# Constant matrix products on TensorE in two idle pieces of a router's first half

## The reference

```python
def reference(x, ctx, ...):
    x = x + slot_attention(layernorm(x), ctx, ...)   # 3 iterations: attention over 32 rows, GRU
    x = x + switch_ffn(layernorm(x), Wg, W1, W2)     # top-1 router, 8 experts
    return x

# the router of switch_ffn, capacity = 512 // 8 = 64
logits = einsum('bnd,de->bne', token_inputs, Wg)
gates = softmax(logits); expert_idx = argmax(gates)
mask = one_hot(expert_idx, 8)
pos = cumsum(mask, axis=1) * mask - mask             # position of the token within its expert
keep = mask * (pos < capacity)
dispatch = keep[..., None] * one_hot(pos, capacity)
expert_inputs = einsum('bnd,bnec->becd', token_inputs, dispatch)
h = gelu(einsum('becd,edh->bech', expert_inputs, W1))
expert_outputs = einsum('bech,ehd->becd', h, W2)
output = einsum('becd,bnec->bnd', expert_outputs, combine)   # combine = dispatch * gate
```

## Time and profile before

| | us |
|---|---|
| median of 3 runs | 147.22 |
| lowest and highest of them | 146.48, 147.29 |
| the profiled execution, whole | 146.29 |
| its span, first to last instruction | 144.5 |
| TensorE busy in the span | 123.9 (86%) |
| VectorE, ScalarE, GpSimd busy | 95.1, 80.3, 33.7 |

### The profile page before, as it was taken

The page is one execution under the profiler, slowest core; times in us unless marked ns, Lnnn a source line. Parts: engine busy times, 40 slices in busy tenths (PEclk is TensorE's granted clock), DMA queues, the critical chain, the costliest instruction groups (busy, mean ns, idle before and its releaser), DMA issues.

```text
span 144.5 us, 2709 instructions
## 1 busy us (share of the span) xinstructions
PE 123.9 (86%) x1007; PEld 92.4 (64%) x1007; DVE 95.1 (66%) x305; ACT 80.3 (56%) x156; POOL 33.7 (23%) x54
## 2 busy tenths in 40 slices
PE   0888999999899899899897833979999999999960
PEld 0684666575475484475474623769998889999730
DVE  2993992399698698796898899955359004124851
ACT  1646592676656746837834818927197246324540
POOL 5670913100500500401300033001400003773000
PEclk9999999999999999999999995599999999999996
DMA  3979970000000000000000000000011001113025
GB/s 110 272 235 351 396 278 0 0 0 2 5 0 0 0 0 0 5 0 2 0 5 0 0 0 0 0 0 5 2 36 39 27 12 40 49 48 93 1 71 145
DMA packets 9198, 8.05 MB, mean 56 GB/s; under 512 B 602, under 2 KB 7029, under 8 KB 9185
## 3 DMA queue, kind: packets, MB, share of 16 engines
q1 hardware_dynamic: 8492, 7.28, 15.5%
q0 software_dynamic: 256, 0.40, 1.1%
q10 hardware_dynamic: 436, 0.20, 0.5%
HBM read 6.43 MB, written 1.57 MB: 55 GB/s over the span
## 4 chain that ended last, share of the span: by engine, by line
PE 75%; ACT 11%; DVE 8%; DMA 2%; issue 1%; ACTq 0%
PE ps L1277 11%; PE ps L1291 11%; PE ps L1116 9%; PE ps L1097 7%; PE ps L1090 7%; PE ps L1198 7%; PE ps L1124 6%; ACT z_b L433 5%; PE ps L1303 3%; PE ps L1073 2%; DMA x_tok<-in_x_dram 2%; PE ps L995 2%; PE ps L1046 2%; PE ps L1056 1%; PE ps L983 1%
## 5 line engine op out<-in xcount | busy, mean ns | idle before, releaser
L1277 PE MATMUL ps<-h,W_t 128*128 128x128 f32 x128 | 16.0, 279 | 0.8 <-ACT h L469 0.8
L428 ACT ACTIVATE ps<-ps,half_b 128x512 f32<-128x512 f32 x12 | 7.9, 661 | 15.6 <-PE ps L1097 15.6
L1277 PEld LDWEIGHTS ps<-h,W_t 128*128 128x128 f32 x128 | 15.0, 192 | 1.8 <-issue 1.7
L1124 PE MATMUL ps<-attn,VW 32*128 32x256 f32 x144 | 12.9, 426 | 3.3 <-DVE ps L710 2.4
L1116 PE MATMUL ps<-h,whhT 128*128 128x256 f32 x48 | 13.5, 403 | 1.2 <-ACT z_b L433 1.2
L1097 PE MATMUL ps<-h,whhT 128*128 128x256 f32 x48 | 13.3, 398 | 0.0
L345 POOL DMA_INDIRECT y_tok<-y_rows,row_of x8 | 8.4, 1044 | 20.2 <-DMA y_rows<-y_sb 18.1
L710 DVE SCALAR_TENSOR_TENSOR ps<-r_b,ps 128x512 f32<-128x512 f32 x12 | 7.8, 693 | 7.6 <-ACT r_b L421 7.6
L1124 PEld LDWEIGHTS ps<-attn,VW 32*128 32x128 f32 x144 | 5.6, 182 | 10.2 <-DVE ps L710 4.8
L1116 PEld LDWEIGHTS ps<-h,whhT 128*128 128x128 f32 x48 | 8.2, 189 | 5.9 <-ACT z_b L433 3.2
L318 POOL TENSOR_SCALAR mse<-attn 128x8 f32<-128x8 f32 x6 | 1.2, 203 | 45.6 <-DVE attn L645 45.6
(11 more groups left out here) (166 smaller groups left out, 262.8 us busy)
## 6 DMA issues: line engine op xcount, KB each, us to landing
W_t<-in_L_ffn_W_dram SPq DMA_DIRECT2D x1, 2048.0 KB, 8.3
x_tok<-in_x_dram SPq DMA_DIRECT2D x4, 256.0 KB, 3.8
out_dram<-h SPq DMA_DIRECT2D x4, 256.0 KB, 2.3
y_rows<-y_sb SPq DMA_DIRECT2D x4, 128.0 KB, 1.8
n_b<-in_L_xattn_gru_whh_dram SPq DMA_DIRECT2D x1, 192.0 KB, 4.0
n_b<-in_L_xattn_gru_wih_dram SPq DMA_DIRECT2D x1, 192.0 KB, 3.8
y_tok<-y_rows,row_of POOLq DMA_INDIRECT x8, 2.5
n_b<-in_ctx_dram ACTq DMA_DIRECT2D x1, 64.0 KB, 2.9
```

Of the source, the lines that this page charges most:

```text
L428: nc.scalar.activation(HV[i], HV[i], ACT.Identity, bias=half_b[:, 2:3]).then_inc(s["hb"], 1)
L1124: last = mm(to[:, hf, :], VW[b][p:p + M, gate * P:(gate + 1) * P], attn[g][p:p + M, :], start=False, stop=True, skip_group_check=True)
L1277: last = mm(hid_bank[e][:, j * BG * CAP:(j + 1) * BG * CAP], W1_t[:, ex_, j * P:(j + 1) * P], rhs, start=True, stop=True)
```

## The change

TensorE gets a helper, `keep_clock(n, to)`, which issues n products of `ones_b` with its own first column, repeated 512 times, into bank `to`. Their results are not read. Five of them stand between `logits(1)` and `positions(0)`, and twelve between `positions(0)` and `dispatch(0)`, all into bank 7. At its start TensorE waits in addition until `ones_b` has been written.

```diff
@@ -972,6 +972,12 @@
             mm = nc.tensor.matmul
             tr = nc.tensor.transpose
 
+            def keep_clock(n, to=2):
+
+                for _ in range(n):
+                    mm(bank[to][:, 0:N], ones_b[:, :], ones_b[:, 0:1].broadcast_to([P, N]), start=True, stop=True)
+
+            pe.wait_ge(dve_set, 2)
             pe.wait_ge(pool_set, 4)
 
             def x_T(b):
@@ -1261,7 +1267,9 @@
             x2_back(1)
             logits(0)
             logits(1)
+            keep_clock(5, to=7)
             positions(0)
+            keep_clock(12, to=7)
             dispatch(0)
             dispatch(1)
 
```

## The result

The changed kernel takes 145.12 us (median of 4, 144.87 to 145.13); beside it the kernel before took 146.85 (median of 4, 146.44 to 147.29). The ratio is 0.9884, with a 95% interval of 0.9848 to 0.9920: 1.2% faster. The forecast was 145.8.

The account below looks back on a forecast made before the run. The prediction took TensorE's dispatch products, run partly at 1.2 GHz, to bound the kernel. Its terms 0 + 0 + 0 - 1.42 us took the median of 147.22 to 145.8 us, with an 8 in 10 range of 144.9 to 147.1.

Parts of the forecast that it names:

- cold products in the dispatch: 16 dispatch products on TensorE, partly at 1.2 GHz, last 6.3 us where about 4.2 us at full clock stand.
- The five and the twelve cost nothing: Five end at 85.2 us, before the mask; twelve end at 88.5, 0.4 us before dispatch(0): each adds 0.
- ScalarE takes over: Before up(0), ScalarE's two copies become the bound by 0.1 us; the second copy moves 1.42 us earlier.
- VectorE's rest for group 1: Rest before VectorE's group 1 work at 99.16 us: 3.02 us, of which 1.6 are left, so the gain stays.
- The profiled execution: Whole kernel in the traced execution: 146.29 us was to become 144.87 us.
- the last one: Step from profiled execution to median of runs: 147.22 us, 0.93 above the profiled one, minus 1.42 gives 145.8.
- would rather have lost more than this one: Argument against the partly saved rival: fewer cold dispatch products in the median execution, saving 0.7 us, 146.5 us, chance 0.16.
- The slow rivals: Clock falls further on, at up(0): 149.2 us, chance 0.07; or before the twelve products: 149.1 us, chance 0.05.
- the cold constants: Clock falls before the twelve, each takes 0.43 us, dispatch(0) starts at 90.8: 149.1 us, chance 0.05.

Follow-up runs that it names:

- the two edits on VectorE: Changed kernel with x2_shift(1) two one-hot tiles earlier on VectorE: 148.07 us; with scale_logits(0) also ahead of dispatch_hot(1): 147.76 us.
- VectorE's edit: Kernel before, without the constants, with x2_shift(1) two one-hot tiles of batch 0 earlier on VectorE: 151.10 us, ratio 1.0015.

## Why the prediction was right, point by point

- What bounds: cold products in the dispatch. Shown: full clock there and 1.49 us less in the stretch, the same in two traces on different chips; without the twelve the low clock and the 10.5 us are back, and with seventeen tiny products in place of the seventeen large ones, too.
- The five and the twelve cost nothing. That was right: `positions(0)` starts 0.06 us behind the mask's end as before, and the dispatch waits for ScalarE. Each takes 0.22 us, forecast 0.23; 0.60 us were spare, forecast 0.4.
- Batch 0 ends 2.13 us after its start and batch 1 2.06, forecast 2.09 each. Batch 1 starts 0.10 us behind x_hi(1), forecast 0.09.
- ScalarE takes over. Shown by its row without a gap and by the two edits on VectorE; with 8 of TensorE's products left out the stretch is still 9.01 us. The size was 1.42 us and is 1.49: I had added the copies end to end, but two in a row last 1.11 us together.
- VectorE's rest for group 1 was to shrink from 3.02 to 1.6 us. It is 1.52, and nothing ate the gain.
- The profiled execution: 144.87 forecast, 145.13 measured; +0.34 of the difference is the first transfer, -0.07 the copies.
- The median: 145.8 forecast, 145.12 measured, 0.68 us less. The step that was off is the last one, in which the 0.93 us between the profiled execution and the median was kept. Of the 0.68, 0.37 are no effect of the change: with a fourth execution the median of the kernel before itself is 146.85 and not 147.22. Against that median the saving is 1.73 us, 0.3 more than forecast. The prediction said that slower executions "would rather have lost more than this one", and that is what the runs on the other chips show: the kernel before spreads with its clock and the changed one hardly does. The rule of the Trainium skill that the monitor behind the clock runs freely ("TensorE: Matmul & The Clock Gate", "What's actually happening") agrees: in three traces of kernels that are alike up to there, the one before, its variant with 8 products fewer and that with VectorE's edit, the clock fell 1.76 us behind the start of `positions(0)`, 1.0 ahead of it and 0.5 ahead of it (at 87.2, 84.4 and 85.9 us).
- The slow rivals were put at 0.07 and 0.05 and did not occur, but both are real: one appears without the five, the other with fewer products in the dispatch. The change stands between two edges that one trace did not show. In that trace the clock fell behind `positions(0)`, which is the exception among the five traces without the five; the prediction's "87.19 is after most of them" was thus weak ground against the cold constants, and the busy share that the five add was the better one.

## What to carry to other kernels

Where TensorE rests a few microseconds ahead of a dense piece on the critical path, look at the granted clock of that piece. Harmless products in the rest are worth what the cold piece costs beyond the next engine's due time. Fill every rest ahead of it, also the short one behind a stretch of transposes or tiny products: filler that starts after the fall runs at half speed (0.43 us a product here, and not 0.22) and itself delays the work. Taking work away from TensorE next to a rest can cost more than it saves, as it did here in the changed kernel, so judge such an edit by the clock of what follows. One trace shows one place of the fall; the next execution may have another.

## What the runs showed of the hardware

- The page prints full clock for the start, but its records of the clock begin only at 12 to 13 us; before that, transposes take twice as long. With seven constants at the start, TensorE's two pairs of L1002 show both speeds, 0.63 and 1.09 us.
- With 8 products fewer in the changed kernel the clock fell at 94.42, after 1.56 us of rest, 1.17 of work and 1.63 of rest. In the changed kernel itself it did not fall with rests of 0.60 and 0.78 us.
- In three traces of kernels alike up to there, the clock fell 1.76 us behind, 1.0 ahead of and 0.5 ahead of the start of the same four products.
- With eight gathers of GpSimd TensorE stands for up to 1 us at a time without a visible wait, in all eleven traces from three chips and in neither of the two from another. Without the gathers the stands and 2.5 us are gone, on one chip.
